# One attention kernel on one core: three bf16 score products in place of one fp32 product, and the preparation jobs in another order

## The reference, cut to what matters

```python
q = _l2norm(q) * q_scale
k = _l2norm(k) * k_scale
sim = jnp.einsum('bhid,bhjd->bhij', q, k) * ATTN_SCALE
sim = sim + dist * slopes
sim = jnp.where(causal_mask, neg, sim)
attn = softmax(sim)
out = jnp.einsum('bhij,bhjd->bhid', attn, v) @ w_out
```

## Time and profile before

| | us |
|---|---|
| median of three runs | 1969.05 (1968.14 to 1970.12) |
| the profiled execution | 1974.28 |
| its span, first to last instruction | 1972.5 |
| prologue, until the first `scores` of turn 0 | 88.05 |
| turns 0 to 14 | 1127.44 (a steady turn: 75.07) |
| turn 15, which prepares nothing | 56.55 |
| the other three stages, from about 1290 on | about 682 |

### The profile page before, as it was taken

One profiled execution on the slowest core, in us unless ns is written; L12 is line 12 of the kernel. 1 busy time (PEld: TensorE's weight loads), 2 busy tenths in 40 slices (PEclk: granted clock), 3 DMA queues, 4 the chain that ended last, 5 costly groups with the idle time before them and its releaser, 6 DMA issues. The chain is left out here.

```text
span 1972.5 us, 28814 instructions
## 1 busy us (share of the span) xinstructions
PE 1632.6 (83%) x8973; PEld 766.2 (39%) x8974; DVE 1096.6 (56%) x2591; ACT 760.9 (39%) x1253; POOL 562.7 (29%) x557
## 2 busy tenths in 40 slices
PE   2699999999999999999999999844973777776777
PEld 1244444444444444443444444443651332232332
DVE  4246556546556655655655655562225666667664
ACT  2345444454454454454454454302431322322221
POOL 1342442442532533533533533152002011110000
PEclk9799999999999999999999999956995887887788
DMA  5501021020220220220220200041110000000000
GB/s 169 159 1 59 16 73 49 25 73 12 62 73 4 70 73 1 73 73 1 73 73 1 73 4 1 1 156 43 47 41 12 6 11 11 11 11 6 0 6 11
DMA packets 109361, 82.02 MB, mean 42 GB/s; under 512 B 5601, under 2 KB 101113, under 8 KB 108974
## 3 DMA queue, kind: packets, MB, share of 16 engines
q1 hardware_dynamic: 107182, 76.15, 12.6%
q0 software_dynamic: 2048, 4.20, 0.7%
HBM read 31.57 MB, written 48.76 MB: 41 GB/s over the span
## 5 line engine op out<-in xcount | busy, mean ns | idle before, releaser
L689 ACT ACTIVATE P<-S,keyb 128x386 f32<-128x386 f32 (+7 forms) x512 | 296.3, 629 | 414.3 <-PE S L490 403.4
L486 PE MATMUL S<-QT,KT 64*128 64x512 f32 (+5 forms) x1792 | 373.1, 473 | 12.7 <-DVE KT L816 11.0
L992 POOL TENSOR_TENSOR rn<-nm,half 128x12 f32<-128x12 f32 x128 | 323.8, 2539 | 23.6 <-DVE nm L753 23.6
L851 DVE TENSOR_TENSOR Psum<-Psum,P 128x1796 f32<-128x1796 f32 (+7 forms) x256 | 287.8, 1124 | 36.2 <-PE O L510 18.4
L1008 POOL TENSOR_SCALAR_AFFINE_SELECT P<-P 128x256 f32<-128x256 f32 (+1 forms) x256 | 117.2, 458 | 620.4 <-ACT P L689 620.3
L510 PE MATMUL O<-P,V 128*64 128x512 f32 (+5 forms) x1536 | 256.7, 437 | 13.9 <-POOL P L1008 11.8
L486 PEld LDWEIGHTS S<-QT,KT 64*128 64x128 f32 (+1 forms) x1792 | 156.5, 178 | 202.9 <-issue 194.0
L162 POOL TENSOR_TENSOR norm_rstd<-norm_vareps,half 128x4 f32<-128x4 f32 x40 | 40.9, 1023 | 481.5 <-DVE norm_vareps L147 481.4
L381 PE MATMUL W<-xT,wts 128*128 128x512 f32 x256 | 142.8, 653 | 15.0 <-DVE QT L812 7.2
L490 PE MATMUL S<-GQ,GK 64*128 64x512 bf16 (+5 forms) x896 | 148.7, 301 | 0.0
L873 DVE TENSOR_TENSOR part<-W,rden 128x512 f32<-128x512 f32 x128 | 82.2, 683 | 91.0 <-PE W L558 91.0
(11 more groups left out here) (214 smaller groups left out, 2221.2 us busy)
## 6 DMA issues: line engine op xcount, KB each, us to landing
xg<-zero SPq DMA_DIRECT2D x16, 1216.0 KB, 8.9
yg<-zero SPq DMA_DIRECT2D x16, 1216.0 KB, 11.9
xT<-xnt SPq DMA_DIRECT2D x16, 512.0 KB, 4.6
wts<-in_w_qkv SPq DMA_DIRECT2D x16, 384.0 KB, 5.6
gu<-in_gu SPq DMA_DIRECT2D x1, 2816.0 KB, 10.3
xb<-xg SPq DMA_DIRECT2D x40, 64.0 KB, 1.8
yg<-yb SPq DMA_DIRECT2D x40, 64.0 KB, 1.6
X<-in_x SPq DMA_DIRECT2D x8, 256.0 KB, 4.5
```

The lines of the kernel that those rows point to most:

```text
L486: nc.tensor.matmul(S[hh][0:m, at + c:at + c + w], KT[d, r, p, jt * P:jt * P + m], QT[d, r, p, Q0[jt] + c:Q0[jt] + c + w], start=True, stop ...
L689: nc.scalar.activation(probs(p, jt)[0:m, hh, 0:n], S[hh][0:m, at:at + n], ACT.Exp, bias=keyb[0:m, r, (2 * p + hh) * NKT + jt:(2 * p + hh) ...
L851: nc.vector.tensor_tensor(x, x, probs(p, jt)[0:m, :, 0:NQ[jt]], ALU.add).then_inc(add_ok, 1)
L992: nc.gpsimd.tensor_tensor(rn[:, c, u], nm[:, c, u], powers, ALU.pow).then_inc(rn_ok, 1)
```

## The change

`QT` and `KT` are kept as two bf16 tiles each, a high and a low part. `scale` writes its fp32 result into a new tile `full`; ACT copies it to the high part (`high`), and DVE subtracts that from `full` to get the low part (`low`). A chunk of `scores` is then three bf16 products (high x high, high x low, low x high) and the bf16 distance product as before. The null keys are split once, before turn 0. The list of jobs gets other steps and banks; four of the eight spreads (S02, S03, S12, S13) become D02, D03, D12, D13 and are done in steps 0a and 0b of the turn that uses them. POOL's four roots of half 1 move from steps 10, 10, 10, 11 to 9, 9, 10, 10. DVE's `parts` of half 1 moves from 12b to 11a. The transfer of the rows of turn t + 2 waits for V1 instead of R0.

```diff
-            AT = {"P00": "0b", "P01": "0b", "P02": "1b", "P03": "2a", "N0": "3b", "T0": "4b", "V3": "4b", "P10": "5a", "P11": "5b",
-                  "P12": "6a", "P13": "6b", "V0": "7a", "V1": "8a", "N1": "8b", "T1": "9b", "V2": "9b", "E0": "10b",
-                  "R0": "11a", "S00": "12b", "S01": "12b", "S02": "13b", "S03": "13b", "E1": "14b",
-                  "R1": "15a", "S10": "16a", "S11": "16b", "S12": "18a", "S13": "18a"}
+            JOBS = {"D02": ("0a", 0), "D03": ("0a", 1), "D12": ("0b", 0), "D13": ("0b", 1), "P00": ("1a", 1), "P01": ("1b", 0),
+                    "P02": ("1b", 1), "P03": ("2a", 0), "N0": ("3b", 0), "T0": ("4b", 0), "V3": ("4b", 1), "P10": ("5a", 0),
+                    "P11": ("5b", 1), "P12": ("6a", 0), "P13": ("6b", 1), "V0": ("7a", 0), "N1": ("7b", 1), "T1": ("8b", 0),
+                    "E0": ("10b", 1), "R0": ("11a", 0), "S00": ("12b", 0), "S01": ("12b", 1), "E1": ("13b", 0), "R1": ("13b", 1),
+                    "S10": ("14a", 0), "S11": ("14b", 1), "V2": ("15a", 0), "V1": ("16a", 1)}
...
-            PREP_BEFORE = (("T1", "E0", ("R0", None), ("S00", "S01")), ("P00", "P02", ("P03", None), ("N0", None)))
+            PREP_BEFORE = (("T1", "E0", ("R0", None), ("S00", "S01")), ("D12", "P02", ("P03", None), ("N0", None)))
...
-                        sp.wait_ge(prep_mm, prepared(t, ROOTS[0]))
+                        sp.wait_ge(prep_mm, prepared(t, "V1"))
...
                     if jt == 0:
-                        for k in SPREAD[1][2 * p:2 * p + 2]:
-                            pe.wait_ge(prep_ev[BANK[k]], emptied(t, k))
+                        pe.wait_ge(low_ok, low_count(t, 1, 2 * p + 1))
...
-                            nc.tensor.matmul(S[hh][0:m, at + c:at + c + w], KT[d, r, p, jt * P:jt * P + m],
-                                             QT[d, r, p, Q0[jt] + c:Q0[jt] + c + w], start=True, stop=False)
+                            nc.tensor.matmul(S[hh][0:m, at + c:at + c + w], KT[d, 0, r, p, jt * P:jt * P + m],
+                                             QT[d, 0, r, p, Q0[jt] + c:Q0[jt] + c + w], start=True, stop=False)
+                        for kpart, qpart in ((0, 1), (1, 0)):
+                            for hh in range(2):
+                                d = slice(hh * DH, (hh + 1) * DH)
+                                nc.tensor.matmul(S[hh][0:m, at + c:at + c + w], KT[d, kpart, r, p, jt * P:jt * P + m],
+                                                 QT[d, qpart, r, p, Q0[jt] + c:Q0[jt] + c + w], start=False, stop=False)
...
+                def high(n, r, c, j):
+                    cycle, k = spread_by(n, c, j)
+                    act.wait_ge(prep_ev[BANK[k]], emptied(cycle, k))
...
+                    nc.scalar.copy(dst, full[:, c, j % 2, :]).then_inc(high_ok, 1)
...
+                    if s in (12, 15):
+                        for j in range(2):
+                            high(n, r, s // 15, j)
...
+                        if s in (2, 3):
+                            for j in (2, 3):
+                                high(t, r, s - 2, j)
...
+                def low(n, r, c, j):
+                    dve.wait_ge(high_ok, low_count(n, c, j))
+                    nc.vector.tensor_tensor(piece(1, r, c, j), full[:, c, j % 2, :], piece(0, r, c, j), ALU.subtract).then_inc(low_ok, 1)
...
                 def prepare(n, r, at):
+                    if at == "9b":
+                        parts(n, 0)
+                    if at == "11a":
+                        parts(n, 1)
...
+                    if at in ("13b", "16b"):
+                        for j in range(2):
+                            low(n, r, int(at == "16b"), j)
...
-                    if at == "12b":
-                        parts(n, 1)
+                def second(t, r, at):
+                    for c, j, k in SECOND:
+                        if AT[k] == at:
+                            scale(t, r, c, j)
+                    if at in ("3b", "7b"):
+                        for j in (2, 3):
+                            low(t, r, int(at == "7b"), j)
...
                     for s in range(STEPS):
+                        second(t, r, f"{s}a")
                         if s == 0 and past:
-                            prepare(t, r, "18a")
                             add(t - 1, 1, NKT - 1)
-                            gather(t - 1, 0, 0)
-                            gather(t - 1, 0, 1)
+                        if s in (1, 2) and past:
+                            gather(t - 1, 0, s - 1)
...
                         if ahead:
                             prepare(t + 1, 1 - r, f"{s}a")
+                        second(t, r, f"{s}b")
                         late = s in (12, 13)
...
-                    for c, u, at in ((0, 0, 5), (0, 1, 6), (0, 2, 7), (0, 3, 8), (1, 0, 10), (1, 1, 10), (1, 2, 10), (1, 3, 11)):
+                    for c, u, at in ((0, 0, 5), (0, 1, 6), (0, 2, 7), (0, 3, 8), (1, 0, 9), (1, 1, 9), (1, 2, 10), (1, 3, 10)):
```

More of the change, by code:

```diff
@@ L223, in build @@
             part = sb("part", [P, 2, 2, 4, D], F32, sc)
+            xnst = part[:, 0]
             S = [ps(f"S{i}", [P, SEQ], F32, sc) for i in range(2)]
@@ L250, in probs @@
                 return Psum[:, p] if jt == 0 else Pr[(jt - 1) % 4][:]
[L255 removed]
[3 rows of a table removed]
[L259 to L260 removed]
+            JOBS = {"D02": ("0a", 0), "D03": ("0a", 1), "D12": ("0b", 0), "D13": ("0b", 1), "P00": ("1a", 1), "P01": ("1b", 0),
[4 rows of a table added]
+            AT = {k: place for k, (place, bank) in JOBS.items()}
+            BANK = {k: bank for k, (place, bank) in JOBS.items()}
+            PREP = tuple(JOBS)
             PROJ = (("P00", "P01", "P02", "P03"), ("P10", "P11", "P12", "P13"))
@@ L263, in build, with spread_by, low_count @@
             VALS = ("V0", "V1", "V2", "V3")
-            SPREAD = (("S00", "S01", "S02", "S03"), ("S10", "S11", "S12", "S13"))
-            PAIR_BEFORE = {"P03": (1, 1), "N0": (1, 2), "T0": (1, 3), "V3": (1, 3), "R0": (0, 1), "S00": (0, 2), "S01": (0, 2),
-                           "S02": (0, 3), "S03": (0, 3)}
-            PREP_BEFORE = (("T1", "E0", ("R0", None), ("S00", "S01")), ("P00", "P02", ("P03", None), ("N0", None)))
+            FIRST = ((0, 0, "S00"), (0, 1, "S01"), (1, 0, "S10"), (1, 1, "S11"))
+            SECOND = ((0, 2, "D02"), (0, 3, "D03"), (1, 2, "D12"), (1, 3, "D13"))
+            PAIR_BEFORE = {"P01": (1, 1), "N0": (1, 2), "T0": (1, 3), "V3": (1, 3), "R0": (0, 1), "S00": (0, 2), "S01": (0, 2),
+                           "E1": (0, 3), "R1": (0, 3)}
+            PREP_BEFORE = (("T1", "E0", ("R0", None), ("S00", "S01")), ("D12", "P02", ("P03", None), ("N0", None)))
+            def spread_by(n, c, j):
+                return (n, f"S{c}{j}") if j < 2 else (n + 1, f"D{c}{j}")
+            def low_count(n, c, j):
+                return 8 * n + 4 * (j // 2) + 2 * c + j % 2 + 1
             def prepared(n, k):
@@ L357, in _ @@
                 pe.sem_inc(out_mm, PAST_OUT)
+                pe.sem_inc(prep_mm, 4)
                 def free_for_prep(n, k, alone):
@@ L436, in roots, with spread, second @@
                     last.then_inc(prep_mm, 1)
-                def spread(n, c, j, alone):
-                    k = SPREAD[c][j]
+                def spread(n, k, c, j, alone):
                     free_for_prep(n, k, alone)
-                    if j == 0:
+                    if k == "S00" or k == "S10":
                         pe.wait_ge(prep_ev[BANK[ROOTS[c]]], emptied(n, ROOTS[c]))
                     nc.tensor.matmul(W[BANK[k]][:], selr[:, j, :], RT[:, 512 * c:512 * c + 512], start=True, stop=True).then_inc(prep_mm, 1)
+                def second(t, at):
+                    for c, j, k in SECOND:
+                        if AT[k] == at:
+                            spread(t + 1, k, c, j, False)
                 def prepare(n, r, lap, at, alone=False):
@@ L463, in prepare @@
                             roots(n, r, c, alone)
-                        for j in range(4):
-                            if AT[SPREAD[c][j]] == at:
-                                spread(n, c, j, alone)
+                    for c, j, k in FIRST:
+                        if AT[k] == at:
+                            spread(n, k, c, j, alone)
                 def scores(t, r, p, jt):
@@ L517, in masses @@
                     pe.wait_ge(add_ok, PAST_ADD + 16 * t + 8 * p + 8)
-                    if ahead:
+                    if ahead or p == 1 and t < TURNS - 1:
                         pe.wait_ge(prep_ev[0], emptied(t + 1 + p, PREP_BEFORE[p][0]))
@@ L533, in masses_turned @@
                         pe.wait_ge(prep_ev[1], emptied(t + 1 + p, PREP_BEFORE[p][1]))
+                    elif p == 1 and t < TURNS - 1:
+                        pe.wait_ge(prep_ev[1], emptied(t + 2, "D13"))
                     elif p == 0:
@@ L566, in turn @@
                         scores(t, r, s // NKT, s % NKT)
-                        if s == 0 and past:
-                            prepare(t, r, lap, "18a")
```

(6 more changed lines are left out.)

55 lines of the change are left out of this document (36 added, 19 removed).

## The result

The changed kernel takes 2053.81 us (median of four runs, 2050.43 to 2053.98) where the kernel before takes 1969.59: 1.0407 times as long, 95% interval 1.0378 to 1.0437. It is slower, as forecast, but by 84 us instead of 35, and outside the range. The profiled execution has a span of 2052.2 us, 79.7 more than before; it took as long as the median, where the one of the kernel before stood some 5 us above its own, and that is the difference between 84 and 79.7.

A forecast was written before the change was run, and what follows sets the result against it. The prediction took PE to bound the turns, busy 70.96 of 75.07 us. To 1969.05 us it added 27 for turns 0 to 14, 10 for the clock and 2 for the prologue, less 4 for turn 15: 2004 us, range 1945 to 2045.

The forecast's parts named there:

- The scores: PE's score products: four passes a chunk instead of five, a gain of 4.4 us a turn (bounds 3.5 and 5.5).
- the old waits: PE's waits in a turn before the change, 0.5 us edges included: 5.3 us, taken off the 75.07 us turn.
- The order followed: All engines' new lists through one turn: new PE waits of 11.5 us, a turn of 76.95 us, 1.9 longer.
- The clock: Falls of PE's clock to 1.2 GHz behind new waits, in most turns: 10 us in all, about ten turns at 1 us.
- partly in slack: Falls of the clock elsewhere than behind step 12, whose stretch lies on the chain: claimed to lie partly in slack.
- the waits of 4.0 and 2.0: New PE waits in each turn: 4.0 us ahead of `outputs` of step 12, 2.0 ahead of step 10's scores.
- the rival with two falls a turn: The clock in full: two falls a turn of 1.6 us, none in slack, 2042 us; chance 0.18.
- Turn 15: The last turn, which prepares nothing and has slack on DVE: 4 us shorter.
- The chain through POOL off the path: Step 9 to 12: the wait of 4.0 gone and its clock falls too, a turn of 72.95, 1934 us; chance 0.17.
- Sum: The whole span: 27 us for turns 0 to 14, 10 clock, 2 prologue, less 4 for turn 15: 35 longer.
- the prologue: Before the first turn: two spread pairs less, but high and low rounds, V2 and V1 added: +2 us (bounds -2 and +4).
- the 1.7 us a turn of contention: A `low` or `add` beside a POOL root, through shared SBUF interfaces: up to 1.7 us a turn more, 2029 in all.

The follow-up runs named there:

- e1: The changed kernel with DVE's `parts` of half 1 back in 12b, behind the two scales, instead of 11a: 1984.47 us.
- e4: The changed kernel with the `low` of steps 3 and 7 behind the add and the norm rows' copy, those of 16b in 15b: 1999.05 us.
- e8: The changed kernel with the reorderings of e1 and e4, and V2 moved from 15a back to 9b: 1935.98 us.
- e2: The changed kernel with 13 extra bf16 products, which nothing reads, in PE's wait of step 12: 2041.68 us.

## Why the prediction was wrong

**The scores.** Four passes for five, as the step said. Of the first load's 0.11 us only 0.03 is left (0.88 less four times 0.213), not half. A turn without a fall has PE busy 65.74 us (e1) where it was 70.96: the gain is 5.2 us, not 4.4, within the bounds. The sum had the old waits too high, though: it took 5.3 us off for them, and 75.07 - 70.96 leaves 4.1. The two errors, 0.8 and 1.2 us, partly cancel, and that the turn came out within 0.6 us is in part luck.

**The order followed.** It held: the waits come to 11.7 us where the forecast had 11.5. From the turn's start at 484.75: the second `outputs` at 23.73 (forecast 23.55), T1 at 40.52 (40.4), the last root at 55.0 (54.9), `rden` at 59.86 (59.65). `low` costs 0.60 from start to start, ACT's `high` 0.62, the roots 4.49 for two beside a DVE that waits. `outputs` of step 12 starts 0.4 us later than forecast (60.07 and 59.65), the rest of the turn is 0.2 longer (17.53 undisturbed and 17.3), and the turn is 77.58 instead of 76.95. Over fifteen turns that is 36 us longer than before instead of 27.

**The clock.** This is the step that failed, by its size: the term of the sum for the falls to 1.2 GHz. The prediction had taken 10 us in all, "about ten turns at 1 us". The turns lost 1202.76 - 1127.44 - 36.3 = 39 us to it. That most turns would fall, and behind step 12, was right; how often and at what price was not. The fall behind step 12 comes in 14 of the 15 turns and costs its full 1.6 us, not 1; four turns have it alone and take 79.2. Six others have it twice as long and a further fall behind the turn's start, and take 81.4 to 81.8; two have both falls at the usual length and take 80.7 and 80.8. In the last two the second fall lies behind step 10's wait and costs next to nothing (79.4 and 79.2), so "partly in slack" was right there. Behind the turn's start no single wait is over 1.6 us, and I had counted only the waits of 4.0 and 2.0 as able to cause a fall. What decides in which turns it comes isn't shown. In the trace before, waits of 1.89 us had done so in two turns, and the rival with two falls a turn, 2042 us, had 0.18; it was nearest, and the measured time lies 12 us beyond it. The Trainium skill ("TensorE: Matmul & The Clock Gate", Why this matters for your kernels) warns of long idle gaps between bursts of matmuls; by that rule every turn pays, and the trace agrees for the 4.04 us of step 12. The falls behind 1.89 us before the change, and behind 1.52, 0.52 and 0.21 us after it, came without a long gap; there the measurement goes further than the warning.

**Turn 15.** Forecast 4 us shorter for its slack on DVE; it became 2.5 longer up to its last `masses` (59.0 and 56.55), with falls of the clock, and with this wait for DVE. The row of PE's timeline at its step 9, and the stretch around it:

```profile
1320.83 0.71 PE L505 MATMUL S<-QT,KT 64*128 64x512 bf16 x2 [2.17 <-DVE KT L875]
...
1319.90:1330.10 10.20, 7.93 (x40) 3.71 (x44) 1.97 (x5) 3.43 (x5) 0.41 (x1) 0.50 0.00 0
```

Slack of the whole turn says nothing of the place: in DVE's order the low parts of D12 and D13 stand behind the adds of four steps and two `gather`, and the second pair's scores wait for them. How much of the 2.5 us is that wait and how much the clock wasn't separated.

**Rivals.** The chain through POOL off the path, forecast at 1934, is what e1 made by hand (1984): the wait of 4.0 went, but `parts` took 1.66 us back, the other new waits and the falls at the turn's start stayed. The rival had the turn at 72.95 by striking one wait and adding nothing; it was 75.10.

**Sum.** 36 + 39 in the turns, 0.45 in the prologue, 3.9 behind turn 14: 79.7 us, where the forecast had 27 + 10 + 2 - 4 = 35. Of the 45 us between them 29 are the clock, 9 the undisturbed turns, 6.5 turn 15, 1.4 what follows it, and the prologue takes 1.5 back.

## What to carry to other kernels

When a change takes work from the engine that bounds a kernel and gives a little to the others, follow every engine's order through one period before counting the gain: here 1.2 us of DVE work in three places, and four POOL instructions with DVE queued behind them, turned a gain of 5.2 us a turn into a loss of 2.4. Then ask of every new wait what the clock will make of it. Here falls behind waits of 1.52, 0.52 and 0.21 us cost as much as the one behind 4.04, though not in every turn, and of what the turns gained in e1, e4 and e8, between a third and three quarters came with the clock and not from the waits that the edits took away. Work that must be done anyway is well placed in a wait that nothing else can shorten: moving V2 there from 15a took 34 us off.

## What the runs showed of the hardware

A cut on POOL, 0.40 us in every undisturbed row, took 2.15 beside DVE's `add` of 1796 columns, and the third root before the change took 3.95 instead of 2.23 beside such an `add`:

```profile
539.74 0.40 POOL L1079 TENSOR_SCALAR_AFFINE_SELECT P<-P 128x256 f32<-128x256 f32 x1
542.56 2.15 POOL L1079 TENSOR_SCALAR_AFFINE_SELECT P<-P 128x256 f32<-128x256 f32 x1 [2.41 <-ACT P L730]
```

In both cases POOL lost about 1.7 us of the 2.0 that the `add` ran. The added `low` instructions have two SBUF inputs as well, and the last cut of a turn, on 2 partitions, shows that they can do the same. The one of step 8 took 0.19 us beside a copy (at 524.48), this one 0.53 beside a `low`:

```profile
562.55 0.68 DVE L875 TENSOR_TENSOR QT<-full,QT 128x512 bf16<-128x512 f32 x1
562.75 0.53 POOL L1079 TENSOR_SCALAR_AFFINE_SELECT P<-P 2x4 f32<-2x4 f32 x1 [1.18 <-ACT P L730]
```

Beside `outputs_out` (L943), which reads one input from PSUM, a cut kept its length: 0.41 us at 504.27. It is not so at every moment either: this root ran beside two `low`, from 522.64 to 523.93, and lost nothing.

```profile
522.25 2.27 POOL L1063 TENSOR_TENSOR rn<-nm,half 128x12 f32<-128x12 f32 x1
```

So a DVE instruction with two SBUF inputs can hold POOL up for most of its own length; the three slow ones above all began while it ran. When exactly it does wasn't worked out. The Trainium skill ("GPSIMD Engine Reference", Specifications) names that contention, and the trace agrees that it exists, but not that each such pair pays. The four roots of half 1 ran beside a DVE that waited, as the prediction had it, so the 1.7 us a turn of contention that it weighed didn't arise. The long cut of step 12 cost nothing, for it ended 0.1 us ahead of `outputs`.

A fall of the clock is not an accident of one turn. In the changed kernel it came 59.6 to 62.9 us behind the start in 14 of 15 turns, always right behind the same wait, and with that wait filled (e2) in none; in e2 all fifteen turns then had one near their start.
